# A two-layer gated cross-attention kernel: context and four weights of the last layer laid out transposed at launch

## What is computed

```python
x = x + tanh(g_xattn[0]) * L0_xattn(layernorm(x), ctx, ctx, mask, wq, wk, wv, wo)   # 32 query, 8 key/value heads of 128, rotary
x = x + tanh(g_ffn[0])   * L0_ffn(layernorm(x), Wg, Wu, Wd)                           # weights and activations fake-quantised
x = x + tanh(g_xattn[1]) * L1_xattn(layernorm(x), ctx, Wq, bq, Wk, bk, Wv, bv)        # 64x64 projections along the token axis
x = x + tanh(g_ffn[1])   * L1_ffn(layernorm(x), W_base, b_base, lora_A, lora_B, router_W, router_b, domain_prior, active)
```

## Time and profile before

| | |
|---|---|
| runs | 798.62, 798.77, 799.89 us; median 798.77 |
| profiled execution, span from first to last instruction | 798.0 us |
| TensorE busy | 786.6 us (99%) |
| VectorE busy | 586.1 us (73%) |
| GpSimd busy | 503.0 us (63%) |
| ScalarE busy | 446.2 us (56%) |
| mean granted clock of TensorE | 0.999 of full |

### The profile page before, as it was taken

How to read it: one execution, slowest core, us unless ns; L and a number is a source line. 1 busy time by engine, 2 the same in 40 slices (tenths; PEclk the granted TensorE clock), 3 DMA queues, 4 the chain that set the end, 5 groups by cost and what they waited for, 6 DMA issues and landing times.

```text
span 798.0 us, 13811 instructions
## 1 busy us (share of the span) xinstructions
PE 786.6 (99%) x5043; PEld 645.2 (81%) x5060; DVE 586.1 (73%) x1098; ACT 446.2 (56%) x844; POOL 503.0 (63%) x429
## 2 busy tenths in 40 slices
PE   8999999999999999999999999999999999999998
PEld 8888888888888888888888888888765777777776
DVE  5867988678888655686666565465899997998874
ACT  4754555444455434444445443334579898888773
POOL 1697577645756764566666456645457885877753
PEclk9999999999999999999999999999999999999999
DMA  9411331431333231733212110167274413213101
GB/s 303 137 67 53 93 93 41 125 84 49 97 87 90 63 102 35 49 89 93 87 40 65 49 47 28 32 68 256 91 184 108 106 41 82 78 48 80 48 15 40
DMA packets 72259, 66.76 MB, mean 84 GB/s; under 512 B 35921, under 2 KB 51505, under 8 KB 71809
## 3 DMA queue, kind: packets, MB, share of 16 engines
q1 hardware_dynamic: 71520, 65.56, 31.6%
q10 hardware_dynamic: 672, 0.33, 0.1%
HBM read 49.04 MB, written 6.34 MB: 69 GB/s over the span
## 4 chain that ended last, share of the span: by engine, by line
PE 93%; DVE 4%; issue 1%; ACT 1%; DMA 0%; POOL 0%; DVEq 0%
PE bank L87 12%; PE bank L88 12%; PE bank L89 12%; PE bank L532 7%; PE bank L527 7%; PE bank L528 7%; PE bank L509 7%; PE bank L653 4%; PE bank L1663 4%; PE bank L1649 3%; PE bank L1615 2%; PE bank L1586 2%; PE bank L1594 2%; PE bank L640 2%; PE bank L1639 2%; PE bank L1640 2%
## 5 line engine op out<-in xcount | busy, mean ns | idle before, releaser
L963 DVE SCALAR_TENSOR_TENSOR x_res<-bank,gate,x_res 128x512 f32<-128x512 f32 x128 | 94.2, 745 | 68.3 <-PE bank L532 68.0
L1249 POOL TENSOR_TENSOR prob<-prob,row_inv 128x512 f32<-128x512 f32 x32 | 33.5, 1046 | 162.8 <-DVE row_inv L959 162.8
L1235 POOL TENSOR_TENSOR rope_swap<-rope_swap,trig 128x512 f32<-128x512 f32 x80 | 105.8, 1322 | 34.8 <-ACT rope_swap L722 34.5
L721 ACT COPY rope_swap<-bank 64x512 f32<-64x512 f32 x80 | 46.7, 583 | 107.2 <-DVE rope_cos L934 107.1
L87 PE MATMUL bank<-xnT_hi,wq_hi 128*128 128x512 f32 x256 | 103.1, 403 | 0.0
L527 PE MATMUL bank<-wo_hi,oT_hi 128*128 128x512 f32 x256 | 101.7, 397 | 1.4 <-DVE x_res L963 0.8
L88 PE MATMUL bank<-xnT_lo,wq_hi 128*128 128x512 f32 x256 | 101.4, 396 | 0.0
L89 PE MATMUL bank<-xnT_hi,wq_lo 128*128 128x512 f32 x256 | 101.1, 395 | 0.0
L528 PE MATMUL bank<-wo_lo,oT_hi 128*128 128x512 f32 x256 | 100.8, 394 | 0.0
L934 DVE TENSOR_TENSOR rope_cos<-bank,trig 128x512 f32<-128x512 f32 x80 | 54.6, 683 | 61.7 <-PE bank L89 61.7
L1241 POOL TENSOR_TENSOR q_rope<-rope_cos,rope_swap 128x512 f32<-128x512 f32 x64 | 84.3, 1318 | 5.0
(11 more groups left out here) (264 smaller groups left out, 2013.8 us busy)
## 6 DMA issues: line engine op xcount, KB each, us to landing
wq_raw<-in_L_xattn_wq SPq DMA_DIRECT2D x16, 512.0 KB, 4.1
wo_raw<-in_L_xattn_wo SPq DMA_DIRECT2D x16, 512.0 KB, 3.9
xn<-in_L_ffn_Wd SPq DMA_DIRECT2D x16, 256.0 KB, 3.2
b_ctx<-in_ctx SPq DMA_DIRECT2D x32, 128.0 KB, 2.7
b_k_twice<-b_qk_hi SPq DMA_DIRECT2D x32, 128.0 KB, 2.4
w_T_dram<-w_out SPq DMA_DIRECT2D x28, 128.0 KB, 2.7
w_T<-w_T_dram SPq DMA_DIRECT2D x2, 1376.0 KB, 18.2
xn<-in_L_ffn_Wg SPq DMA_DIRECT2D x10, 256.0 KB, 3.8
```

The lines of the kernel that those rows point to most:

```text
L963: dve.scalar_tensor_tensor(out=K.x[:, t, :], in0=wo_ps[t % 2][:, :], scalar=K.gate[:, 0:1], in1=K.x[:, t, :], op0=ALU.mult, op1=ALU.add).t ...
L1235: pool.tensor_tensor(out=sw, in0=sw, in1=sin_b, op=ALU.mult).then_inc(s_rope, 1)
```

## The change

The host lays out five arrays at launch: the context as ctx_T (two halves of 512 tokens, four chunks of the model dimension each, that dimension on the partitions), W_base, the attention weights of the last layer (query and key side by side, twice; value twice on a diagonal) and lora_B transposed. The kernel loads them in that layout, and TensorE's transposes of them go, with the copies that took them out of PSUM where no high part is needed (bT). High parts and rests are taken from the raw tiles in SBUF, by chunk instead of by token tile. The first half of the context is four loads, the second half one load of 1 MB. k0 is one item of 12 matmuls of 512 columns that waits chunk by chunk. The first key weights get their high part on VectorE and their rest on GpSimd. The order of the first items becomes k0, v0, v1, k1, v2, x tiles 0 to 3, v3. On ScalarE, base_high_part(0) is behind prior_logarithm, and base_high_part(1) behind oT_hi(31); VectorE's slots are as before. lora_B is one load in place of four with 32-byte rows.

```diff
@@ SyncE
-            for t in range(4):
-                load_ctx(t)
+            for n in range(DC):
+                load_ctx(n)
             load_wv(0)
             sp.dma_start(wv_first, wv_piece(1)).then_inc(s_wv_first, 16)
-            for t in range(4, NT):
-                load_ctx(t)
+            sp.dma_start(ctx_raw[1][:, :, :], ctxT_dram[1].rearrange("c p t -> p c t")).then_inc(s_ctx_in[DC], 16)
@@ TensorE, head
                 for c in range(DC):
-                    mm = mm3(pe, out[:, lo:lo + n], wh[:, c, cols], wl[:, c, cols], ah[:, c, tok], al[:, c, tok], c == 0, c == DC - 1)
-                if part != 0:
-                    mm.then_inc(s_proj, 1)
+                    if kind == "k" and G == 0:
+                        pe.wait_ge(s_ctx_lo, hf * DC + c + 1)
+                    mm = mm3(pe, out[:, :], wh[:, c, cols], wl[:, c, cols], ah[:, c, tok], al[:, c, tok], c == 0, c == DC - 1)
+                mm.then_inc(s_proj, 1)
...
-            for n in range(UT):
-                transpose_tile(n)
-            for part in range(2):
-                pe.wait_ge(s_tr_lo, 2 * part + 2)
-                item(0, 0, part)
-            item(0, 1)
-            for n in range(UT, NT):
-                transpose_tile(n)
-            item(0, 2)
+            for pos in range(5):
+                item(0, pos)
+            for t in range(UT):
+                transpose_tile(t)
+            item(0, 5)
...
@@ TensorE, turn
-                if U == 2 * NPAIR - 1:
-                    base_T(1)
-                    base_T(2)
...
-                if U == 2 * NPAIR - 2:
-                    qkv_T()
-                    base_T(0)
 
             run_slots(slot)
-            base_T(3)
-            b_T()
@@ ScalarE, head
-            wk_piece(0)
-            for n in range(UT):
-                hi_tile(n)
+            for n in range(DC):
+                ctx_hi_piece(n)
             wv_piece(0)
             act.wait_ge(s_wv_first, 16)
             act.copy(wv_hi[:, 2:4, :], wv_first).then_inc(s_wkv_hi, 1)
+            ctx_hi_piece(DC)
             evacuate(0, 0)
+            for n in range(DC + 1, 2 * DC):
+                ctx_hi_piece(n)
             evacuate(0, 1)
-            for n in range(UT, NT):
-                hi_tile(n)
             evacuate(0, 2)
@@ ScalarE, turn
             def base_high_part(c):
-                act.wait_ge(s_w_ps, W_BASE + c)
-                act.copy(M.base_hi[:, c, :], base_ps[c][:, :]).then_inc(s_w_hi, 1)
+                act.wait_ge(s_proj, len(ALL))
+                act.wait_ge(R1.s_in, 16 * R1.n_loads)
+                act.copy(M.base_hi[:, c, :], R1.base[:, c, :]).then_inc(s_w_hi, 1)
...
-                    if U == 2 * NPAIR - 1:
-                        base_high_part(1)
                     act.wait_ge(s_av, U + 1)
...
                     if U == 2 * NPAIR - 2:
                         qkv_weights()
-                        base_high_part(0)
                         first_split_hi(0)
                         first_split_hi(1)
                         prior_logarithm()
+                        base_high_part(0)
+                    if U == 2 * NPAIR - 1:
+                        base_high_part(1)
@@ VectorE, head
-            lo_tile(0)
-            split(wk_raw[:, :, :], wk_hi[:, :, :], wk_lo[:, :, :], s_wkv_hi, s_wkv_lo, 1)
-            for n in range(1, UT):
-                lo_tile(n)
-            split(wv_first, wv_hi[:, 2:4, :], wv_lo[:, 2:4, :], s_wkv_hi, s_wkv_lo, 3)
+            dve.wait_ge(s_wk_in, 16)
+            dve.tensor_copy(wk_hi[:, :, :], wk_raw[:, :, :]).then_inc(s_wk_first, 1)
+            for n in range(DC):
+                ctx_lo_piece(n)
+            split(wv_first, wv_hi[:, 2:4, :], wv_lo[:, 2:4, :], s_wkv_hi, s_wkv_lo, 2)
             dve.wait_ge(K.s_gate_in, 16)
             times_cos(0, 0)
+            for n in range(DC, 2 * DC):
+                ctx_lo_piece(n)
             bn(0)
...
@@ the launch
+    ctx = np.asarray(inputs["ctx_4096"]).reshape(B * S, D).T
...
+    return [("ctx_T", ctx.reshape(DC, P, 2, HALF).transpose(2, 0, 1, 3)),
+            ("base_T", base.reshape(DC, P, D).transpose(1, 0, 2)),
+            ("qk_T", np.tile(np.concatenate([wq, wk], axis=1), (2, 1))),
+            ("v_T", v_two),
+            ("lora_b_T", np.asarray(inputs["L1_ffn_lora_B"]).transpose(0, 2, 1).reshape(P, D)),
+            ("rope_table", rope_table())]
```

More of the change, by code:

```diff
@@ L156, in attention_block @@
         sem = cx.sem
-        s_ctx_in = [sem(f"s_ctx_in{i}") for i in range(NT)]
+        s_ctx_in = [sem(f"s_ctx_in{i}") for i in range(DC + 1)]
+        s_ctx_hi, s_ctx_lo = sem("s_ctx_hi"), sem("s_ctx_lo")
+        s_wk_in, s_wk_first = sem("s_wk_in"), sem("s_wk_first")
         s_x_in = [sem(f"s_x_in{i}") for i in range(4)]
@@ L580, in low_T @@
                 pe.matmul(trans[:, HD:HD + E_ACT], M.spread[:, :], M.sel_e[:, :], start=True, stop=True).then_inc(s_w_lowT, 1)
-            def b_T():
-                pe.wait_ge(s_w_lo, 2)
-                for c in range(DC):
-                    mm = pe.transpose(proj[0][:, c * P:(c + 1) * P], R1.b[:, c, :], K.ident[:, :])
-                mm.then_inc(s_w_ps, 1)
             def low_b_select():
-                pe.wait_ge(s_w_lo, 4)
-                pe.wait_ge(s_w_bT_sb, 1)
-                pe.matmul(proj[1][:, :], M.sel[:, :, :].rearrange("p a n -> p (a n)"), M.bT[:, :], start=True, stop=True
+                pe.wait_ge(s_proj_read, len(ALL))
+                pe.matmul(proj[1][:, :], M.sel[:, :, :].rearrange("p a n -> p (a n)"), R1.b[:, :], start=True, stop=True
                           ).then_inc(s_w_ps, 1)
@@ L1104, in base_low_part @@
                 dve.wait_ge(s_w_hi, c + 1)
-                dve.tensor_tensor(out=M.base_lo[:, c, :], in0=base_ps[c][:, :], in1=f32(M.base_hi[:, c, :]), op=ALU.subtract
+                dve.tensor_tensor(out=M.base_lo[:, c, :], in0=R1.base[:, c, :], in1=f32(M.base_hi[:, c, :]), op=ALU.subtract
                                   ).then_inc(s_w_lo, 1)
@@ L1337, in block1_raw @@
     R, sb = Raw1(), area.take
-    R.qkv = [sb(f"l1_raw{i}", [S, S]) for i in range(3)]
+    R.qk, R.v = sb("l1_raw_qk", [P, P]), sb("l1_raw_v", [P, P])
     R.a = sb("l1_raw_a", [P, D])
-    R.b = sb("l1_raw_b", [P, DC, P])
+    R.b = sb("l1_raw_b", [P, D])
     R.r = sb("l1_raw_r", [E_ALL, D])
@@ L1344, in block1_raw @@
     R.s_in = cx.sem("s_l1_in")
[L1345 removed]
+    R.n_loads = 4 + 1 + 4 + 3 + 1 + 1
     return R
@@ L1360, in load_block1 @@
         load(W.bv[h * S:(h + 1) * S, :], a["L1_xattn_bv"].unsqueeze(1))
-    for c in range(DC):
-        load(R.b[:, c, :].rearrange("p (e r) -> p e r", e=E_ALL),
-             a["L1_ffn_lora_B"][:, c * P:(c + 1) * P, :].rearrange("e p r -> p e r"))
-    for i, name in enumerate(("L1_xattn_Wq", "L1_xattn_Wk", "L1_xattn_Wv")):
-        load(R.qkv[i][:, :], a[name])
+    load(R.b[:, :], a["lora_b_T"])
+    load(R.qk[:, :], a["qk_T"])
+    load(R.v[:, :], a["v_T"])
     load(R.act_i[:, :], a["L1_ffn_active"].partition_broadcast(P))
 def load_base(sp, R, a):
-    sp.dma_start(R.base[:, :, :], a["L1_ffn_W_base"].rearrange("(c p) h -> p c h", p=P)).then_inc(R.s_in, 16)
+    sp.dma_start(R.base[:, :, :], a["base_T"]).then_inc(R.s_in, 16)
 def late_buffers(cx, K):
@@ L3333 @@
     arrays, aps = {}, {}
-    for name, value in [*inputs.items(), ("rope_table", rope_table())]:
+    for name, value in [*inputs.items(), *laid_out(inputs)]:
         arrays["in_" + name] = v = np.ascontiguousarray(value)
```

197 lines of the change are left out of this document (83 added, 114 removed).

## The result

| | before | after |
|---|---|---|
| median (us) | 799.33 (4 runs) | 809.07 (808.33 to 812.1, 4 runs) |
| ratio | | 1.0128 [1.0114, 1.0141] |
| profiled execution: time; span | span 798.0 | 809.32; 807.1 |
| TensorE busy | 786.6 | 786.3 |
| mean granted clock | 0.999 | 0.991 |

A forecast was written before the change was run, and what follows sets the result against it. TensorE carried 93% of the chain, but ScalarE was taken to set the head and VectorE's queue the turn. Span 798.0 - 0.3 + 5.0 + 1.4 = 804.1, median 0.77 over it: 804.9 us; range 801.8 to 807.2.

The forecast's parts named there:

- The bound before: Turn of the two layers, 564 to 578 us: VectorE's queue sets the pace; head: ScalarE's run from 20.14 to 28.59.
- The turn's waits: At the turn, VectorE's rests wait for ScalarE's later base copies: +3.65 at output 30, +5.0 us in all.
- The clock: At the turn, TensorE's clock falls in the first gap, slowing eight matmuls of tiles 2 and 3: +1.4 us.
- rival 2: At the turn, the clock is low again behind TensorE's second gap, too: 806.7 us; chance 0.12.
- Removed at the turn: TensorE's 23 transposes removed at the turn lay under other work: 0, against -2.3 us if each counted.
- The head: First 30 us: first query projection at about 29.2 in place of 29.48, -0.3 us; bounds -1.6 and +0.8.
- the landing of wq: Head: the first query weights land at 20.14 and that does not move, the loads ahead being bound by bytes.
- the fall that I had named: Head: a clock fall ahead of k0 would cost it up to 2.4 us, but nothing in the end.
- the lock that the prediction's first part tells of: Head: SBUF as an exclusive lock, its loser blocked for the whole instruction; up to 1.3 us for k0, hidden.
- The sum: Whole kernel: span 798.0 - 0.3 + 5.0 + 1.4 = 804.1, median 0.77 over the span: 804.9 us.
- rival 1: At the turn, TensorE's clock stays up through the gaps: 803.5 us; chance 0.28.
- rival 3: Head and turn: removed transposes count (-1.7 and -2.3) and VectorE's order does not matter: 794.8 us; chance 0.07.

The follow-up runs named there:

- both gaps filled: Changed kernel plus transposes of the identity where TensorE waits, 30 at output 30, 8 and 16 around tile 0 of output 31: 805.38 us, ratio 1.0074.
- first gap filled: Changed kernel plus 30 transposes of the identity on TensorE ahead of tile 2 of output 30, none later: 809.91 us, ratio 1.0117.
- second gap filled: Changed kernel plus 8 and 16 transposes of the identity on TensorE around tile 0 of output 31, none earlier: 810.27 us, ratio 1.012.
- the first experiment: Changed kernel with both of ScalarE's base copies, base_high_part(0) and (1), back where they were before the change: 800.23 us, ratio 1.0007.
- the fastest kernel: Changed kernel with both base copies back, 34 warm-up transposes for 11, two x statistics ahead of context rests 5 to 7: 797.86 us, ratio 0.9974.
- early rests: Changed kernel, base copies and two rests taken in slot 30, 34 warm-up transposes, two x statistics ahead of context rests: 798.03 us (800.59 without the head edits).

## Why the prediction was right and where it failed

**The bound before.** Right for the turn: it hung on VectorE's queue, and it was enough to move two instructions of ScalarE that VectorE's queue waits for. Wrong for the head, as told below.

**The turn's waits: +5.0, bounds 4.7 and 5.3; measured 4.8.** Right, step by step: base copy at 570.68 (said 570.7), VectorE's rest at 571.31 (571.3), the accumulation at 571.92 (571.9), tile 2 at 572.72 (572.6). The second wait is 2.03 (some 2), and 1.71 with both gaps filled. These starts are the changed kernel's; with the clock kept up TensorE went on at 582.66, where 582.5 was said.

**The clock: +1.4, bounds 0 and 3.2; measured 4.15.** This is the step that failed, in two places: the first fall cost 2.5 and not 1.4, and the second, which I put at nothing, some 1.6.
The first fall was right: at 571.4, some 2.3 us behind the end of tile 1. Its length was not. I took 3.4 us from the launch, and the low stretch is 6.8 us: all 12 matmuls of tiles 2 and 3 ran slow, and not the first eight. The profiled executions show both lengths, and longer ones, by the lengths and means of their stretches: 6.8 twice after the change, once with the first copy back and once with the first gap filled; 3.4 in the kernel before with ScalarE's order, with the second gap filled and with VectorE's rests moved; 13.6 once, with 34 warm-up transposes. One sample stood for a quantity with several values. And the term did not follow from its own premise: eight steps of 0.23 at double are 1.8 us, not 1.4. With a low stretch of 3.4 us the same place lost 1.5.
Second, it fell twice. That was rival 2, at 0.12. I argued from the idle time of the second gap alone. But the low clock came back also where TensorE stood only 1.22, 0.68 and 1.17 us (first copy back, fall at 576.8) and the transposes that had lain there were gone. I had counted these at 0, since other work hid them. That is true of their time: with both copies back the turn is 18.00 beside 18.58. But they had also kept TensorE active, and the runs speak for it, though not with one voice. For it: with the old transposes in place the profiled execution had no second fall, and with 16 new ones in those places none at all. Against it as the whole cause: the other three executions of each of these two kernels had 0.995 to 0.996, and their clocks were low somewhere. The Trainium skill (TensorE: Matmul & The Clock Gate, Part 4) says that a transpose doesn't count as busy for the clock in the way a matmul does; the trace disagrees: with 30 transposes alone in the first gap the granted clock stayed 1.00.
The columns of TensorE alone make up this cost, as I had counted them. VectorE's third and fourth accumulations do wait for slow tiles, 0.92 and 1.08, but VectorE then stands 2.03 for the second base copy all the same, and tile 3 of TensorE starts without a wait.

**Removed at the turn: 0.** Right for their time, within 0.6 us, and wrong for what they may have held up. The covers that I named hold: 1.22, 0.68 and 1.17 us of idle time now stand where transposes stood.

**The head: -0.3; measured -0.17.** The size is luck: two errors cancel, and both stand in rows of TensorE.
First, the bound. I had ScalarE's run behind the landing of wq set the first query projection, with TensorE waiting at the x transposes. But in the kernel before TensorE stands nowhere between 7.82 and 29.48; its own queue sets the head. The x transposes start when v2 ends, at 24.06 before and at 23.35 after:

```profile
24.06 1.47 PE L464 MATMUL bank<-ident,xn 128*128 128x128 f32 x12
```

```profile
23.35 1.47 PE L450 MATMUL bank<-ident,xn 128*128 128x128 f32 x12
25.54 0.39 PE L81 MATMUL bank<-wv_hi,ctxT_hi 128*128 128x256 f32 x1 [0.28 <-ACT rope_swap L668]
```

From the start of v0 to the first query projection TensorE takes 18.64 us before (10.84 to 29.48, and as much in the kernel before with ScalarE's order), 17.33 after, and 17.05 to 17.76 in every other kernel with the new layout. So the 16 transposes of 13.82 to 15.48, 1.66 us, do count, but for this wait of 0.28 and less than 0.1 besides.
Second, v0 starts at 11.98 and not at 10.84, since k0 ran at the lower level, the fall that I had named, priced at up to 2.4 for k0, and then put at nothing:

```profile
3.71 0.42 PE L566 MATMUL bank<-ident 128*128 128x128 f32 x1
6.95 0.79 PE L81 MATMUL bank<-ctxT_hi,wk_hi 128*128 128x512 f32 x1 [2.82 <-POOL wk_lo L1153]
7.54 0.63 PE L82 MATMUL bank<-ctxT_lo,wk_hi 128*128 128x512 f32 x1
7.97 0.63 PE L83 MATMUL bank<-ctxT_hi,wk_lo 128*128 128x512 f32 x1
...
11.98 0.28 PE L81 MATMUL bank<-wv_hi,ctxT_hi 128*128 128x256 f32 x1
```

With steps of 0.43 it ended at 12.0. So the head is 17.33 - 18.64 = -1.31 by the transposes and 11.98 - 10.84 = +1.14 by the later start. In the kernels with 34 warm-up transposes k0 runs at full pace: v0 starts at 10.90, 10.84 and 10.55, and the first query projection at 28.66, 27.89 and 27.96. With 11 of them, the nine profiled executions of the new layout start v0 anywhere between 11.42 and 12.84 and the projection at 29.4 in the mean; the two with the old head have 29.48 and 29.80. Hundredths of a single execution, such as this -0.17, mean nothing.
That the landing of wq does not move can't be told: ScalarE's copy of it starts at 18.41 to 19.62 with the new layout, but at 19.44 also in the kernel before with only ScalarE's order changed.
The rest of wk took 1.65 us on GpSimd beside VectorE (said 1.3), and VectorE's three context rests beside it 2.54 where three took 1.91 before; that fits the lock that the prediction's first part tells of, on both of its sides.

**The sum.** I put the median 0.77 over the span. In every run here 2.1 to 2.3 us lie around the span, the kernel before included. Its profiled execution, with a span of 798.0, was simply a slower one than the three that gave the median. That misplaced the forecast by nothing as a difference (9.1 between spans, 9.7 between medians), but the base was not what I took it for. By terms: -0.17 in the head, +0.4 in the long middle (scatter), 4.8 of waiting and 4.15 of clock. The lower end of the range holds a slip: rival 1 with a head of -1.6 is 802.2, not 801.8.

**The rivals.** Rival 2 was the right one, undersized. Of rival 3 (faster, the order does not matter) the second half fell with the first experiment. Its claim that the transposes count in time fell at the turn and held in the head, where the slow k0 took the gain back.

## What to carry to other kernels

When a copy moves behind table loads or another slow step, look for the instruction of another engine that waits for it, and at what is queued behind that instruction; here moving either of the two cures it. Work that is hidden and worthless in time may still be part of what holds TensorE's clock up: before removing it, add up what is left of TensorE's activity in that place, and price the low clock at a stretch longer than the one sample at hand. To find what bounds a stretch, look first whether TensorE stands in it at all; another engine's run without a gap is not yet a bound. Judge such a change by several executions: the runs of one kernel here differ by 4 us and more together with their clock.

## What the runs showed of the hardware

**The clock falls by chance, in a place with less work.** Of 56 executions of the kernel before whose clock is on record none had a mean granted clock under 0.998. Of 55 executions of the five kernels that have the new layout and in which VectorE no longer waits for a base copy, 14 had less. Three are of the ten of the fastest kernel, with 0.997; two are of the 12 with early rests, with 0.993 and 805.43 and 806.26 us, where the median is 800.59. This agrees with the removed transposes having held it up, but these kernels differ in other ways too. In the profiled execution of the fastest it fell in the turn:

```profile
573.00:576.00 3.00, 3.00 (x8) 2.12 (x9) 2.28 (x4) 0.81 (x2) 1.97 (x5) 0.55 0.00 0
576.00:577.00 1.00, 1.00 (x5) 0.77 (x4) 1.00 (x4) 0.00 (x0) 0.00 (x0) 0.65 0.50 139
```

Both base copies stand there as before, and no idle time is over 1.22 us. Its turn is 19.1, beside 18.0 in the kernel with both copies back, where the clock stayed up.

**It falls in the middle of the run, too, where all the kernels have the same code.** In two profiled executions TensorE waited 2.52 and 2.11 us for VectorE at 340 us (0.81 in that of before), and the clock was low behind it: for 3.4 us with the first gap filled, and for 10.2 with VectorE's rests moved, whose rows these are:

```profile
340.29 0.50 PE L515 MATMUL bank<-wo_hi,oT_hi 128*128 128x512 f32 x1 [2.11 <-DVE x_res L904]
```

```profile
344.00:350.00 6.00, 6.00 (x34) 5.39 (x34) 2.62 (x4) 1.66 (x4) 0.00 (x0) 0.50 0.28 86
```

TensorE is busy all through this stretch and still at the lower level. From the first query projection to the attention of unit 30 it takes 539.63, 5.6 more than the changed kernel, which covers the 4.9 between its 805.61 and the median of 800.75. What made VectorE late there I did not settle.

**The granted clock of the profile does not show the launch.** For 7 to 11 us after the change it reads 1.00, while k0's steps take 0.43 us as in any stretch at 0.50. At the start of a trace the pace of the matmuls is the thing to read.
